# Pl passes directly behind their Ph passes, folds and embedding lows on GpSimd, and a paced first tile

## What is computed

```python
for idx, (W, b) in enumerate(params):            # W: (39, 39 or 64, 128)
    z = jnp.einsum('bhd,bkd,hks->bsd', x0, xk, W) + b[None, :, None]
    z = jax.nn.relu(z)
    if idx != n_layers - 1:
        half = z.shape[1] // 2
        xk = z[:, :half, :]
        direct.append(z[:, half:, :])
    else:
        direct.append(z)
logit = jnp.sum(jnp.concatenate(direct, axis=1), axis=-1)
...
h = jnp.concatenate([z, dense_ctx], axis=1)
h = jnp.maximum(h @ W_top1 + b_top1, 0.0)
h = jnp.maximum(h @ W_top2 + b_top2, 0.0)
y = h @ W_top3
```

## Time and profile before

| | us |
|---|---|
| median of three runs | 2707.83 (2706.82 to 2710.12) |
| the profiled execution as a run | 2715.18 |
| its span, first to last instruction | 2713.4 |

### The profile page before, as it was taken

One profiled execution on the slowest core, in us unless ns is written; L12 is line 12 of the kernel. 1 busy time (PEld: TensorE's weight loads), 2 busy tenths in 40 slices (PEclk: granted clock), 3 DMA queues, 4 the chain that ended last, 5 costly groups with the idle time before them and its releaser, 6 DMA issues.

```text
span 2713.4 us, 32379 instructions
## 1 busy us (share of the span) xinstructions
PE 2539.3 (94%) x8718; PEld 1594.4 (59%) x8718; DVE 2273.5 (84%) x1982; ACT 1624.5 (60%) x2055; POOL 1702.2 (63%) x1094
## 2 busy tenths in 40 slices
PE   0899999999999999999999999999999999999989
PEld 0456566566666656666666666666666666666645
DVE  1588888988889888888998888889888888988881
ACT  1566566666566666656666666666666666566653
POOL 6567567575766757576675757667575766744440
PEclk6899999999999999999999999999999999999999
DMA  2667567567666756765665676576567557656730
GB/s 68 144 130 153 108 140 151 121 127 158 134 126 139 152 118 130 158 133 120 146 145 122 132 158 126 122 151 142 121 136 158 125 123 152 140 122 133 157 77 1
DMA packets 214674, 352.48 MB, mean 130 GB/s; under 512 B 34373, under 2 KB 47546, under 8 KB 214546
## 3 DMA queue, kind: packets, MB, share of 16 engines
q1 hardware_dynamic: 194675, 346.95, 59.2%
q0 software_dynamic: 19968, 5.15, 1.9%
HBM read 346.86 MB, written 5.12 MB: 130 GB/s over the span
## 4 chain that ended last, share of the span: by engine, by line
PE 65%; issue 12%; ACT 9%; DVE 8%; POOL 4%; DMA 1%; ACTq 0%; SPq 0%; DVEq 0%; another core or an unknown queue 0%; POOLq 0%
PE ps L762 21%; PE ps L752 16%; PE ps L773 13%; PE ps L742 9%; ACT Ph L433 4%; DVE P L605 4%; PE ps L737 3%; POOL emb L352 3%; ACT sq L425 2%; DVE ps L605 2%; POOL Pl L358 2%; DVE Pl L610 1%; DVE dir L634 1%; PE ps L879 1%; PE ps L730 1%
## 5 line engine op out<-in xcount | busy, mean ns | idle before, releaser
L358 POOL TENSOR_TENSOR Pl<-P,Ph 128x1024 fp32r<-128x1024 f32 x448 | 1091.8, 2438 | 766.5 <-ACT Ph L433 729.3
L605 DVE TENSOR_TENSOR P<-xb,ps 128x1024 f32<-128x1024 f32 x768 | 928.1, 1214 | 43.5 <-DMA xb<-x_dram 36.1
L762 PE MATMUL ps<-Ph,wh 128*128 128x512 f32 x1920 | 895.8, 472 | 31.5 <-ACT Ph L433 31.3
L610 DVE TENSOR_TENSOR Pl<-ps,Ph 128x1024 fp32r<-128x1024 f32 x512 | 626.8, 1224 | 247.6 <-ACT Ph L433 231.0
L433 ACT ACTIVATE Ph<-ps 128x1024 fp32r<-128x1024 f32 x512 | 522.4, 1020 | 452.2 <-DVE ps L605 382.5
L773 PE MATMUL ps<-Pl,wh 128*128 128x512 f32 (+1 forms) x1920 | 718.4, 454 | 10.0 <-POOL Pl L358 10.0
L352 POOL DMA_INDIRECT emb<-tbl_in,idx x624 | 607.0, 973 | 165.5 <-issue 144.7
L762 PE MATMUL ps<-Ph,wl 128*128 128x512 f32 x1792 | 706.6, 394 | 0.0
L605 DVE TENSOR_TENSOR ps<-xb,ps 128x1024 f32<-128x1024 f32 x512 | 627.5, 1226 | 32.3 <-issue 18.5
L433 ACT ACTIVATE Ph<-P 128x1024 fp32r<-128x1024 f32 x448 | 475.0, 1060 | 271.9 <-DVE P L605 246.4
L752 PE MATMUL ps<-P,wp 128*128 128x512 f32 x1280 | 611.2, 599 | 3.5 <-DVE P L605 3.5
(11 more groups left out here) (56 smaller groups left out, 675.6 us busy)
## 6 DMA issues: line engine op xcount, KB each, us to landing
xb<-x_dram SPq DMA_DIRECT2D x1280, 256.0 KB
emb<-tbl_in,idx POOLq DMA_INDIRECT x624
x_dram<-rows_sb SPq DMA_DIRECT2D x64, 78.0 KB
xb<-w_in SPq DMA_DIRECT2D x15, 128.0 KB
xb<-wt_in SPq DMA_DIRECT2D x2, 512.0 KB, 9.0
xb<-dense_in SPq DMA_DIRECT2D x1, 768.0 KB, 5.3
wp<-w_in SPq DMA_DIRECT2D x5, 128.0 KB
xb<-w0a_in SPq DMA_DIRECT2D x1, 409.5 KB
```

Of the source, the lines that this page charges most:

```text
L358: pool.tensor_tensor(Pl[:, h_slot(ref, c, k)], P[:, p_slot(ref, c, k)], Ph[:, h_slot(ref, c, k)], ALU.subtract).then_inc(low_pool, 1)
L605: dve.tensor_tensor(p, xb[:, x], xk.unsqueeze(1).broadcast_to([128, 2, N]), ALU.mult)\
L610: dve.tensor_tensor(Pl[:, h_slot(ref, c, k)], p_ps, Ph[:, h_slot(ref, c, k)], ALU.subtract)\
L762: pe.matmul(z_of(c, k), w[:, q, j, :], Ph[:, h_slot(ref, c, k), j, :], start=k in (L1B, L2) and i + j == 0, stop=False)
```

## The change

- PE: `late` is gone. The Pl pair of a step stands directly behind its Ph passes. The second pass of the pair takes all 128 rows in steps 0 and 14 too.
- VectorE: the folds and the embedding's low part are gone from it.
- GpSimd: has them now. The low part reads the rounded embedding from a buffer of its own (`emb_h`), so that ScalarE's full copy no longer waits for it. The gathers are 9, 9, 12 and 9 in chunks 0 to 3; in chunk 1 they stand in the steps up to 9.
- ScalarE: square 1 is at step 7 instead of 8, ahead of the z1 copy. Rounded and full copy of the embedding are both at step 15 of chunk 1 (before 12 and 16).
- SyncE: in the first tile the spreads of pairs 4 to 9 and of the next chunk wait for products.

```diff
-SQUARE_LAG, CONTRACT_LAG = 3, 3
+SQUARE_AT = [6, 7, 10, 12, 14, 16, 18]
+CONTRACT_LAG = 3
 DIRECT0_AT, UPPER0_AT, LOWER0_AT, RELU2_AT, DIRECT1_AT, RELU1_AT = 0, 1, 2, 4, 7, 8
-HIGH_AT, LOW_AT, FULL_AT = 12, 14, 16
-FOLD0A_AT, FOLD0_AT, FOLD1A_AT, FOLD1_AT = 13, 13, 8, 8
+HIGH_AT, FULL_AT, LOW_AT = 15, 15, 17
+FOLD0A_AT, FOLD0_AT, FOLD1A_AT, FOLD1_AT = 14, (12, 14, 16, 18), 8, (6, 8, 10, 12)
...
-            for c in range(2):
-                write_rows(0, c)
-                for p in range(PRE if c else PAIRS):
-                    spread(c, p)
+            write_rows(0, 0)
+            for p in range(PRE):
+                spread(0, p)
+            write_rows(0, 1)
+            for p in range(PRE, PAIRS):
+                sp.wait_ge(products, p - PRE + 1)
+                spread(0, p)
+            for p in range(PRE):
+                sp.wait_ge(products, PAIRS - PRE + p + 1)
+                spread(1, p)
...
+            def low_emb(T):
+                pool.wait_ge(emb_high, T + 1)
+                pool.tensor_tensor(emb2[:, :, 1, :], emb[:, :, :].rearrange("p f d -> p d f"),
+                                   emb_h[:, :, :].rearrange("p f d -> p d f"),
+                                   ALU.subtract).then_inc(emb_low, 1)
+
+            def fold(buf, col, done, T, stage, last, half):
+
+                if stage:
+                    pool.wait_ge(done, FOLDS * T + stage)
+                if stage == 0:
+                    o_, x, y = buf[:, 1], buf[:, 0], buf[:, 1]
+                elif stage == 1:
+                    o_, x, y = buf[:, last], buf[:, half], buf[:, last]
+                elif stage == 2:
+                    o_, x, y = buf[:, last], buf[:, 1], buf[:, last]
+                elif stage == 3:
+                    o_, x, y = buf[:, last, N // 2:], buf[:, last, :N // 2], buf[:, last, N // 2:]
+                else:
+                    o_ = feat[:, col, bass.ds(T * TB, TB)]
+                    x, y = buf[:, last, N // 2:N // 2 + TB], buf[:, last, N // 2 + TB:]
+                pool.tensor_tensor(o_, x, y, ALU.add).then_inc(done, 1)
+
+            def fold0(T, stage):
+                fold(dir0, 0, folds0, T, stage, 3, 2)
+
+            def fold1(T, stage):
+                fold(dir1, 1, folds1, T, stage, 2, 0)
...
             take_ids(0)
             for f in range(NF):
                 gather(f)
-            pool.wait_ge(emb2_ready, 1)
-            pool.wait_ge(gathered, 16 * NF)
-            take_ids(1)
+            low_emb(0)
+
+            def next_ids(T):
+
+                pool.wait_ge(emb_full, T)
+                pool.wait_ge(emb_low, T)
+                take_ids(T)
+
+            next_ids(1)
...
                     todo = list(fields[c])
-                    each = -(-len(todo) // len(GATHER_AT))
+                    slots = [k for k in GATHER_AT if c != 1 or k < FOLD0A_AT - 4]
                     for k in range(STEPS):
                         if KIND[k] == "G" and (CPT * ref + c, k) in STEPSET:
                             low(T, ref, c, k)
-                        elif k in GATHER_AT:
-                            for f in todo[:each]:
+                        if k in slots:
+                            n = -(-len(todo) // len(slots[slots.index(k):]))
+                            for f in todo[:n]:
                                 gather(f)
-                            todo = todo[each:]
-
-            a, b = NF // 3, 2 * NF // 3
-            first, second, third = range(0, a), range(a, b), range(b, NF)
-            tile(0, 0, (range(early, 32), range(32, NF), first, second))
+                            todo = todo[n:]
+                        if c == 0 and not first and k in FOLD1_AT:
+                            if k == FOLD1_AT[0]:
+                                pool.wait_ge(z2_read, T * CPT)
+                            fold1(T - 1, FOLD1_AT.index(k) + 1)
+                        if c == 2 and k == FOLD1A_AT:
+                            pool.wait_ge(z2_read, T * CPT + 2)
+                            fold1(T, 0)
+                        if c == 1 and k == FOLD0A_AT:
+                            pool.wait_ge(z0_read, T * CPT + 2)
+                            pool.wait_ge(z1_read, T * CPT + 2)
+                            fold0(T, 0)
+                        if c == CPT - 1 and k in FOLD0_AT:
+                            if k == FOLD0_AT[0]:
+                                pool.wait_ge(z0_read, T * CPT + CPT)
+                                pool.wait_ge(z1_read, T * CPT + CPT)
+                            fold0(T, FOLD0_AT.index(k) + 1)
+                        if c == 1 and k == LOW_AT and not last:
+                            low_emb(T + 1)
+
+            cuts = (0, 12, 21, 30, NF)
+            third, fourth, first, second = (range(a, b) for a, b in zip(cuts, cuts[1:]))
+            tile(0, 0, (range(early, 30), range(30, NF), third, fourth), first=True)
             with pool.Fori(1, TILES - 2) as T:
-                tile(T, 1, (third, (), first, second))
-            tile(TILES - 2, TILES - 2, (third, (), (), ()))
-            tile(TILES - 1, TILES - 1, ((), (), (), ()))
+                tile(T, 1, (first, second, third, fourth))
+            tile(TILES - 2, TILES - 2, (first, second, (), ()))
+            tile(TILES - 1, TILES - 1, ((), (), (), ()), last=True)
+            pool.wait_ge(z2_read, chunks)
+            for stage in range(1, FOLDS):
+                fold1(TILES - 1, stage)
...
-                act.activation(emb2[:, :, 0, :].bitcast(F32R), emb[:, :, :].rearrange("p f d -> p d f"), ACT.Copy)\
-                    .then_inc(emb_high, 1)
+                act.activation(emb_h[:, :, :], emb[:, :, :], ACT.Copy).then_inc(emb_high, 1)
 
             def full_emb(T):
-                act.wait_ge(emb_low, T + 1)
                 act.activation(emb2[:, :, 0, :], emb[:, :, :].rearrange("p f d -> p d f"), ACT.Copy)\
-                    .then_inc(emb2_ready, 1)
+                    .then_inc(emb_full, 1)
...
-                        if k - SQUARE_LAG in SUM_AT and not no0:
-                            t = SUM_AT.index(k - SQUARE_LAG)
+                        if k in SQUARE_AT and not no0:
+                            t = SQUARE_AT.index(k)
                             square(T, aux + 1 + t, t)
                         if c == 1 and not last:
                             if k == HIGH_AT:
-                                act.wait_ge(aux_ready, T * PER["aux"] + aux + 1)
                                 high_emb(T + 1)
                             if k == FULL_AT:
+                                act.wait_ge(aux_ready, T * PER["aux"] + aux + 1)
                                 full_emb(T + 1)
...
-            def low_emb(T):
-                dve.wait_ge(emb_high, T + 1)
...
-            def fold(buf, col, done, T, stage, last, half):
...
-                dve.tensor_tensor(o_, x, y, ALU.add).then_inc(done, 1)
...
-                q, twice = SPL.index(k), k in SINGLE_STEPS
+                q = SPL.index(k)
                 if KIND[k] == "G":
                     pe.wait_ge(low_pool, upto(T, ref, ONPOOL, c, k))
                 else:
                     pe.wait_ge(low_dve, upto(T, ref, ONDVE, c, k))
                 for j in range(2):
-                    rows = slice(0, K1 if twice and j else 128)
-                    m = pe.matmul(z_of(c, k), wh[rows, q, j, :], Pl[rows, h_slot(ref, c, k), j, :], start=False,
+                    m = pe.matmul(z_of(c, k), wh[:, q, j, :], Pl[:, h_slot(ref, c, k), j, :], start=False,
                                   stop=stop and j == 1)
                 m.then_inc(split_done, 1)
 
-            def contract(T, ref, c, k, late):
+            def contract(T, ref, c, k):
 
                 group_end = k in (L1B - 1, STEPS - 1)
                 if KIND[k] == "P":
-                    plain(T, ref, c, k, group_end and not late)
+                    plain(T, ref, c, k, group_end)
                 else:
                     high(T, ref, c, k)
-                if late:
-                    low(T, ref, *late, group_end and KIND[k] == "P")
-                if KIND[k] == "P":
-                    return None
-                if group_end:
-                    low(T, ref, c, k, True)
-                    return None
-                return c, k
+                    low(T, ref, c, k, group_end)
...
-                            pe.wait_ge(emb2_ready, T + 1 + (c + 2) // CPT)
+                            pe.wait_ge(emb_full, T + 1 + (c + 2) // CPT)
+                            pe.wait_ge(emb_low, T + 1 + (c + 2) // CPT)
...
-                        late = contract(T, ref, c, k, late)
-                assert not late
+                        contract(T, ref, c, k)
```

More of the change, by code:

```diff
@@ L136, in build @@
         emb = sb("emb", [TB, NF, D])
+        emb_h = sb("emb_h", [TB, NF, D], F32R)
         emb2 = sb("emb2", [TB, D, 2, NF])
@@ L204, in build @@
         emb_low = sem("emb_low")
-        emb2_ready = sem("emb2_ready")
+        emb_full = sem("emb_full")
         settled = sem("settled")
```

(37 more changed lines are left out.)

20 lines of the change are left out of this document (removed).

## The result

The changed kernel takes 2754.65 us (median of four runs, 2751.86 to 2755.79) against 2708.51 for the kernel before: 1.0169, 95% interval 1.0151 to 1.0187, so 46 us slower. The forecast was 2744 us and +36. Its profiled execution has a span of 2749.9 us, where the sum had given 2749.

What follows compares the result with a forecast made beforehand. PE was taken to bound the kernel, every chunk opening waiting for it. About +2.4 us a tile over 14.5 tiles, +35 us, and +1 put 36 us on the median: 2744 us, range 2703 to 2785.

Steps and rivals of the forecast that it cites:

- the sum: All terms added: about +2.4 us a tile over 14.5 tiles, +35 us, and +1, span from 2713.4 to about 2749.
- What bounds the kernel: At chunk openings: ScalarE waits for PE's last square contraction, so what PE loses inside a chunk is added.
- Term (1): Pl passes directly behind Ph passes: PE waits 0.6 us at step 4, some 1.1 at step 7; chunk 39.68 us.
- The two chains: Beside PE: from the opening to Pl of step 4 (t 11.06), and from the z1 copy to Pl of step 7 (18.09).
- Term (2): 64-row pair made 128-row, steps 0 and 14: 0.40 us each; step 14 gains, step 0 disappears in step 4's wait.
- Term (3): Square 1 at step 7, ahead of the z1 copy: removes a 0.70 us gap, but nothing more comes of it.
- Term (4): Folds and embedding lows leave VectorE: all second halves of chunks taken as PE's alone, gain already in the 39.68 us.
- Term (5): GpSimd's new queue: folds and lows fit, but five gathers before Pl of step 4 make chunk 1 take 41.4 us.
- The margins: GpSimd's Pl of step 11, chunk 0, ends at 26.2, wanted at 26.6; steps 13 and 15, chunk 3, fit alike.
- Term (6): Head, tail, first tile: embedding low gains 1 us, first loop turn costs 1, last folds cost 1; +1 us in all.
- The median: Median of three runs before the change, 2707.8 us; the forecast put 36 us on it, giving 2744 us.
- the count of 14.5 tiles: Tiles multiplied by about +2.4 us: the first tile lacks the pattern and the last is cut short; +35 us.

## Why the prediction was right

- *What bounds the kernel* (every opening waits for PE; what PE loses inside a chunk is added): held. ScalarE still waits for PE at the openings, for 3.0 to 3.6 us.
- *Term (1)*, 39.68 us a chunk: 39.68, 39.78 and 39.78 in chunks 0, 2 and 3. The two chains ran as laid out, pair by pair: 11.12, 13.85, 18.15 foretold, 11.10, 13.90, 18.17 measured. The run with steps 4 and 7 late shows that these waits carry most of the loss, 122 of 155 us. The waits for Pl came in 200 places, three a chunk and not two, and sum to 160 us where I had near 100 or more: that of step 0 is one more (0.52 us long in this chunk). As foretold it costs nothing in this kernel, since PE would wait for step 4 anyway.
- *Term (2)*, 0.40 a chunk in the changed kernel: 0.37 to 0.38. The kernel before shows the same 0.39 to 0.40 behind the pass of step 0, but what both passes bring there is 0.27 to 0.39 a chunk, since PE meets ScalarE's round of step 4. Twice 0.40, as I had for that kernel, was too high.
- *Term (3)*, no gain from the earlier square: held in chunks 0 and 2; 0.13 in chunk 3, and chunk 1 stays open.
- *Term (4)*, all second halves are PE's: held in the changed kernel. Its reason was right for the changed kernel only. With the direct order in the kernel before (2793 instead of 2755 us) VectorE held PE up even though PE was late.
- *Term (5)*: Pl of step 11 in chunk 0 was to start at 23.8 and end at 26.2; it ended at 26.0. The margins held in the changed kernel and not in the faster ones. A fold of 512 on GpSimd was a little dearer than the estimate, and the embedding low, whose rows are read with a stride, nearer its upper bound (groups by form, mean ns of one):

```profile
L390 POOL TENSOR_TENSOR dir<-dir 128x512 f32<-128x512 f32 x96 | 126.5, 1318 | 4.0 <-ACT dir L509 2.9
L371 POOL TENSOR_TENSOR emb<-emb,emb_h 128x624 f32<-128x624 f32 x16 | 39.5, 2471 | 2.1 <-ACT emb_h L471 2.1
```

  The five gathers cost 1.7 us in chunk 1, as foretold, and their own experiment gave it back (1.66).
- *Term (6)*, +1 us: wrong, and in the other direction. The first tile's chunk 0 opens 2.9 us earlier (98.7 instead of 101.6); but in the experiments on the changed kernel, which have the same head but for their edits, it opens between 97.0 and 101.1, so this is scatter in part. GpSimd did not stand still in its first turn: that tile, the second, took 160.6 us where it took 164.9, the opposite of my +1. From the opening of the last tile on both kernels take 221.9 and 221.8 us, so nothing of the +1 for the folds at the end shows in the time.
- *The sum*: a tile as in the earlier trace rows takes +2.6 for the +2.4 foretold. That the spans moved by 36.5 where I had 36 is partly luck. The 13 tiles behind the second took 43.2 us more, 3.3 each and not 2.4: besides the 2.6 of a usual tile the changed kernel has more single long chunks, above all chunks 1 (one of 46.6 us). Against these 12 us stand the head, the second tile and the end, which together came out 12 us lower than term (6) and the count of 14.5 tiles had them.
- *The median* moved by 46 us and the profiled spans by 36.5. I had put the move of the spans on the median; the one profiled execution of the kernel before was 7 us slower than its median, that of the changed kernel 3 us faster. That is the 10 us between 2744 and 2755.

## What to carry to other kernels

Lay two chains against each other and put a consumer at the first place at which its input is ready, kind by kind: an operand that a slow engine makes needs another step's work ahead of it, one that a fast engine makes doesn't. When an engine with a rising share in the chain of waits has the same work in a faster variant, it was not the bound: its latency stood uncovered. The share itself is no measure of what is lost: it was 48% at 2755 us, 34% at 2600, and 6% at 2586 and at 2574. And an engine's spare time has to be priced in the order that will use it, since the relief of VectorE, with the gathers, squares and loads that moved with it, was worth 92 us with the pairs a step later (0.9926 to 0.9587, 128 rows in both) and 14 us with the pairs direct (1.0298 to 1.0246, 64 rows in both). Part of that difference is what the crowded gathers of chunk 1 cost, 15 us with late pairs and 35 with direct ones by the ratios.

## What was not expected of the hardware

A matmul pass with a 64-row operand between 128-row passes costs more than one with all rows: 0.37 to 0.38 us a chunk in the changed kernel, and 0.39 behind the pass itself in the kernel before. The weight load of the 64-row pass starts only after 0.37 us of idling, so it isn't hidden behind the pass ahead of it. Why it starts late is not shown.

GpSimd stands still for 2 to 3 us (once 5.8) ahead of a gather, for nothing that the profile shows, four times in each of the two kernels, in the changed one some 460 us apart (timeline of GpSimd of the changed kernel):

```profile
794.97 0.94 POOL L360 DMA_INDIRECT emb<-tbl_in,idx  x1 [3.16 <-issue]
```

In the changed kernel this one falls into a chunk 1 that took 46.6 us instead of 41.4; the others, at 1256, 1730 and 2190, fall into chunks that are 1.4 to 2.0 us longer than the median of their kind. The cause was not looked for, and stays open.
